# A decoder layer on one core: the self-attention's slot table rearranged, and two small operations moved from VectorE to GpSimd

## The chip, the cores and the metric

One core of one Trainium2 chip runs the whole program. The metric is device time in microseconds of that core. The kernel before was timed three times: 860.68, 863.87 and 865.61 us, median 863.87. Its profiled execution took 868.03 us, of which the profile spans 866.3 us. Engines are called by the profile's names: PE is TensorE, DVE is VectorE, ACT is ScalarE, POOL is GpSimd, SP is the sync engine, which here only issues transfers.

## The reference

Input `x` is 8 batches of 256 tokens of 512 numbers. Three stages follow each other: causal self-attention with 16 heads of 32 numbers, cross-attention with one head over 256 context rows and the tokens' own keys, and a mixture of 8 experts with one expert per token. The change touches the first stage alone:

```
h   = layernorm(x)                       # 8 x 256 x 512
qkv = h @ w_qkv                          # q, k, v of 16 heads x 32
p   = softmax(causal(q @ k.T / sqrt(32)))
x   = x + (p @ v) @ w_out
x   = x + cross_attention(layernorm(x)); x = x + experts(layernorm(x))
```

## The kernel before, in words

Float32 products are made in three passes: each operand is split into a high part, that TensorE multiplies fast, and a low part, the difference (`three_pass`, L51). ACT makes the high part out of PSUM by a cast, DVE the low part by a subtraction; for the probabilities and for v, POOL splits the rest once more (L322 to L324, L335 to L337).

The order of work is written out by hand. `self_attention` (L61) runs each batch in 16 slots, one for each head; all engines run the same list of slots and hand over by semaphores. In slot h, PE computes the scores S(h) of head h (L457). DVE takes the row maxima out of PSUM (L576), ACT takes the exponentials (L398). Two slots later PE transposes the probabilities (T, L470), ACT casts them (`pt_part[0]`, L408), one slot later DVE subtracts (`pt_rest`, L585) and POOL splits the rest (L335, L337). Every fourth slot, five slots behind the last head of a group of four, PE multiplies a group's probabilities by v (AV, `heads_by_values`, L488), and right behind it spreads the reciprocals of the row sums over PSUM by a product with the identity (L495). Before that DVE takes the reciprocals (L600) and copies them 32 wide (`rinv`, L603), three slots behind the last head. ACT copies the spread reciprocals (`r_sb`, L412), DVE multiplies (L590), ACT casts the product to `ot_hi` (L418), DVE subtracts to `ot_lo` (L594). `r_sb`, `o_sb` and `rinv` are one buffer, so that these steps follow each other strictly.

Beside heads, slots hold projection jobs on PE (`SLOTS`, L131): q0 to q3 and k0 to k3 (queries and keys of the four groups), u0, u1 and w0, w1 (values of the first and second half of the heads), X0, X1 (transposes of the normalised input), y0, y1 (output projection of the batch before). The job banks are two; a job waits until the job two before it has been taken out of PSUM. q and k go from `qk` to `stack` by SP transfers inside SBUF, since S wants high and low parts on top of each other: 12 transfers of 128 KB for half of the heads (`stack_half`, L252, L257), the second half when k3 is out, the first when k1 is. S waits for a head's own three transfers of those.

What the batches share: q0 to q2, k0 to k2, X and u of batch n+1 are made in batch n; a prologue makes those of batch 0 and, at its end, u0 and u1. Layer norm of the next batch is on DVE in slots 0 and 2 (L521 to L532), with one power on POOL in slot 1 (L315).

PE's order in a slot is S, AV, jobs, T. DVE's is the low part of the job before, maxima, `pt_rest`, output steps, reciprocals. ACT's is exponentials, the slot's own job, `pt_part`, output steps.

Of the kernel before, what the change touches and what calls it, by code (L numbers as in the profile page):

```python
# [60 lines left out]
def self_attention(nc, ident, x, w_qkv, w_out, x1, xin, xr, x1_out, x1_last_out, x1_first_in,  # L61
# [13 lines left out]
    HEAD_IN = 16 * 3  # L75
    NPROB, NPT, NREST = 4, 8, 4
    with ExitStack() as cx:
# [21 lines left out]
        r_sb = o_sb = rinv[:].rearrange("p q j d -> p (q j d)")  # L99
# [8 lines left out]
        stack = sb("stack", [3 * HD, 2, HG, 2, GH, S], F32R)  # L108
# [11 lines left out]
        stacked = [[sem(f"stacked_{half}_{j}") for j in range(HG)] for half in range(2)]  # L120
# [14 lines left out]
        PROLOGUE = ["X0", "X1", "q0", "k0", "q1", "k1", "q2", "k2", "u0", "u1"]  # L135
# [44 lines left out]

        def head_at(slot, lag, n):
# [16 lines left out]
        def v_at(j, n):  # L198

            return TB + n * V_JOBS + int(j[1]) + (0 if j[0] == "w" else TB)  # L200
# [44 lines left out]
        def _(sp):  # L245
# [6 lines left out]
            def stack_half(half):  # L252
                for j in range(HG):
                    for r, parts in enumerate((slice(0, 3, 2), slice(1, 3), slice(0, 4, 3))):
                        dst = stack[HD * r:HD * (r + 1), half, j, :, :, :].bitcast(F32)
                        src = qk[HD * j:HD * (j + 1), half, parts, :, :].bitcast(F32)
                        sp.dma_start(dst.rearrange("p w g s -> p w (g s)"),  # L257
                                     src.rearrange("p w g s -> p w (g s)")).then_inc(stacked[half][j], 16)

            def batch(n):  # L260

                wait(sp, job_ev, job_at("k3", n) + 1)
                sp.sem_inc(tick_sp, 1)
                if isinstance(n, int) and n == 0:
                    sp.wait_ge(w_split, 3)
                    sp.wait_ge(wo_split, 2)
                wait(sp, s_done, n * H)
                stack_half(1)
# [11 lines left out]
                if has("k1", n):  # L280
                    wait(sp, job_ev, job_at("k1", n) + 1)
                    sp.sem_inc(tick_sp, 1)
                    wait(sp, s_done, n * H + H // 2)
                    stack_half(0)
# [4 lines left out]
            wait(sp, job_ev, job_at("k1", -1) + 1)  # L289
            sp.wait_ge(w_split, 2)  # L290
            stack_half(0)
# [9 lines left out]
        def _(pool):  # L301
# [25 lines left out]
            def slot(n, h):  # L327
                if h == 1 and head_at(h, 0, n) is not None and (not isinstance(n, int) or n < B - 1):
                    next_rstd(n + 1)
# [9 lines left out]
                before = h - LO_JOB_LAG  # L339
                for j in jobs_of(before, n) if before >= 0 else jobs_of(H + before, n - 1 if isinstance(n, int) else n):  # L340
                    of = n if before >= 0 else n - 1
                    if j[0] in "uw" and not (isinstance(of, int) and of < 0):
                        v_lower_parts(j, of)

# [5 lines left out]
            for j in PROLOGUE:  # L350
                if j[0] == "u":
                    v_lower_parts(j, -1)
# [13 lines left out]
        def _(act):  # L366
            def evac(j, n):
# [3 lines left out]
                if j in ("q0", "q2"):  # L371
                    for s in stacked["q0 q2".split().index(j)]:
                        wait(act, s, (n + 1) * HEAD_IN)
                if j == "u0":
                    wait(act, av_done, n * G + GH if not isinstance(n, int) or n >= 0 else 0)
# [7 lines left out]
            for j in PROLOGUE:  # L383
# [4 lines left out]
                if j == "u0":  # L388
                    act.wait_ge(consts, CONSTS)
                evac(j, -1)  # L390

            def slot(n, h):
                e = head_at(h, 0, n)
# [7 lines left out]
                for j in jobs_of(h, n):  # L401
                    if j not in LATE:
                        evac(j, n)
                t = head_at(h, T_LAG, n)
                if t is not None:
                    act.wait_ge(t_done, n * H + h - T_LAG + 1)
                    wait(act, av_done, groups_before(h, T_LAG + NPT, n) + 1)
                    nc.scalar.copy(pt_part[0][:, t % NPT, :], t_ps[t % 2][:, 0:3 * P]).then_inc(pt_hi_done, 1)  # L408
                g = group_at(h, R_LAG, n)
                if g is not None:  # L410
                    act.wait_ge(r_done, groups_before(h, R_LAG, n) + 1)
                    nc.scalar.copy(r_sb, o_ps[g % 2][:, 1, :]).then_inc(rs_done, 1)  # L412
                g = group_at(h, ON_LAG, n)
                if g is not None:
                    if g == 0 and not (isinstance(n, int) and n < 1):
                        act.wait_ge(job_done, job_at("y1", n) + 1)
                    act.wait_ge(on_done, groups_before(h, ON_LAG, n) + 1)
                    nc.scalar.copy(ot_hi[:, g, :], o_sb).then_inc(ot_hi_done, 1)  # L418

# [11 lines left out]
        def _(pe):  # L431
            def job(j, n):
# [3 lines left out]
                if j == "q0":  # L436
                    pe.wait_ge(job_ev, job_at("X1", n) + 1)
                if j == "y0":
                    pe.wait_ge(ot_done, n * G)
# [4 lines left out]
            for j in PROLOGUE:  # L444
                if j in ("q0", "k0", "u0"):
                    pe.wait_ge(w_split, "qku".index(j[0]) + 1)
                job(j, -1)

            def slot(n, h):
                s = head_at(h, 0, n)  # L450
                if s is not None:
                    g, j = divmod(s, HG)
                    if s % (H // 2) < HG:
                        pe.wait_ge(stacked[g // GH][j], (n + 1) * HEAD_IN)
                    wait(pe, mx_done, n * H + h - 1)
                    for q in range(TB):
                        m = nc.tensor.matmul(s_ps[s % 2][:, q, :], stack[:, g // GH, j, 0, g % GH, q * P:(q + 1) * P],  # L457
                                             stack[:, g // GH, j, 1, g % GH, :], start=True, stop=True)
                    m.then_inc(s_done, 1)
                g = group_at(h, AV_LAG, n)  # L460
                if g is not None:
                    heads_by_values(g, h, n)
                for j in jobs_of(h, n):
                    job(j, n)
                t = head_at(h, T_LAG, n)
                if t is not None:
# [4 lines left out]
                    m.then_inc(t_done, 1)  # L471

            def heads_by_values(g, h, n):

                before, of = groups_before(h, AV_LAG, n), n if h >= AV_LAG else n - 1
                if g == 0:
                    pe.wait_ge(v_done, v_at("u1", of - 1) + 1)
# [34 lines left out]
        def _(dve):  # L512
            def norm_stats(k):
# [6 lines left out]
                for t in range(TB):  # L520
                    nc.vector.bn_stats(stats[:, t, :], xin[:, t, :]).then_inc(ln_dve, 1)  # L521
                for t in range(TB):
# [21 lines left out]
            norm_stats(0)  # L544
            norm_apply(0)
            for j in PROLOGUE:
# [5 lines left out]
                if j == "u0":  # L552
                    dve.wait_ge(consts, CONSTS)
                evac(j, -1)

            def slot(n, h):
                before = h - LO_JOB_LAG
                for j in jobs_of(before, n) if before >= 0 else jobs_of(H + before, n - 1 if isinstance(n, int) else n):
                    of = n if before >= 0 else n - 1
                    if isinstance(of, int) and of < 0:  # L560
                        continue
                    if j in LATE:
                        dve.wait_ge(job_done, job_at(j, of) + 1)
                        dve.wait_ge(xr_in, 16 * of)
                        xt = xr[:, int(j[1]), :]
                        nc.vector.tensor_tensor(xt, bank(j, of)[:, :], xt, ALU.add).then_inc(job_ev, 1)
                    else:
                        evac(j, of)
                s = head_at(h, 0, n)
                if s is not None:  # L570
# [9 lines left out]
                    m.then_inc(mx_done, 1)  # L580
                t = head_at(h, LO_LAG, n)
# [6 lines left out]
                if g is not None:  # L588
                    dve.wait_ge(rs_done, groups_before(h, ON_LAG, n) + 1)
                    nc.vector.tensor_tensor(o_sb, o_ps[g % 2][:, 0, :], r_sb, ALU.mult).then_inc(on_done, 1)  # L590
                g = group_at(h, OT_LAG, n)
                if g is not None:
                    dve.wait_ge(ot_hi_done, groups_before(h, OT_LAG, n) + 1)
                    nc.vector.tensor_tensor(ot_lo[:, g, :], o_sb, ot_hi[:, g, :].bitcast(F32),  # L594
                                            ALU.subtract).then_inc(ot_done, 1)
                g = group_at(h, RINV_LAG, n)
                if g is not None:
# [3 lines left out]
                    dve.wait_ge(rinv8_done, before + 1)  # L601
                    wait(dve, ot_done, before)
                    nc.vector.tensor_copy(rinv[:], free_ap(rinv8[:, g, :, :], 0, [[HG, TB], [1, HG], [0, HD]]))\  # L603
# [938 lines left out]
```

## Time and profile before

| | |
|---|---|
| median of 3 runs | 863.87 us (860.68 to 865.61) |
| profiled execution, its span | 868.03 us, 866.3 us |
| self-attention on PE | from 8.2 us to 391.98 us |
| busy over the span | PE 88%, DVE 61%, ACT 43%, POOL 36% |
| stretch 214 to 272 us, steady self-attention: busy of 58 us | PE 52.61, DVE 41.27, ACT 36.10, POOL 35.89; granted clock 1.00 |

A row of the order-of-time view has the start, the duration, the engine, the line of the kernel, the operation, output and inputs with sizes, and how many instructions are merged; in brackets stands how long the engine was idle before and who released it. Durations overlap: the next instruction may start before the last has ended, so the price of a step is here the distance from its start to the next start. Matmul ends are modelled. The granted clock is 1.00 at 2.4 GHz and 0.50 at 1.2 GHz.

### The profile page before, as it was taken

The page shows a single profiled execution, that of the slowest core. Times are in us where ns is not written, and L with a number is a line of the kernel's source. Part 1 is how long each engine was busy: PE and PEld are TensorE (multiplying, and loading weights), DVE is VectorE, ACT ScalarE, POOL GpSimd, SP SyncE. Part 2 cuts the span into 40 slices and gives each one's busy share as a digit, 9 for nine tenths or more (in the row PEclk, how much of TensorE's full clock was granted, in tenths as well). Part 3 has the DMA queues.
Part 4 walks back from the last instruction along what each step waited for, and adds up shares of the span by engine and source line. Part 5 has one row for each costly group of instructions (what it writes and reads, how often), then busy time and mean ns, then how long its engine had stood idle before and what let it go on. Part 6 is the DMA issues. An engine that isn't in the chain of part 4 may idle for free. (4 is left out here: it accounts for less than half of the span.)

```text
span 866.3 us, 19948 instructions
## 1 busy us (share of the span) xinstructions
PE 762.7 (88%) x6424; PEld 688.1 (79%) x6425; DVE 529.1 (61%) x1557; ACT 370.4 (43%) x1145; POOL 312.2 (36%) x456
## 2 busy tenths in 40 slices
PE   4798989898989999757999999999999985739995
PEld 4787979888888888646899998989899974637884
DVE  4678685868686867546565655556464533834664
ACT  4476675757575767534423232313133220622221
POOL 3376574757565656641000101010101101124662
PEclk9999999999999999879999999999999997868998
DMA  9643343444444434306712425060502111765630
GB/s 345 147 114 94 105 101 106 93 118 93 116 93 118 93 94 115 101 1 208 286 52 72 99 23 113 8 121 20 101 30 67 59 15 49 168 163 152 199 122 24
DMA packets 49575, 90.90 MB, mean 105 GB/s; under 512 B 11390, under 2 KB 11518, under 8 KB 49408
## 3 DMA queue, kind: packets, MB, share of 16 engines
q1 hardware_dynamic: 43872, 77.80, 34.2%
q0 software_dynamic: 5664, 12.61, 4.7%
q8 instruction: 21, 0.34, 0.2%
q14 instruction: 18, 0.15, 0.1%
HBM read 51.95 MB, written 18.77 MB: 82 GB/s over the span
## 5 line engine op out<-in xcount | busy, mean ns | idle before, releaser
L398 ACT ACTIVATE prob<-prob,nmax 128x128 f32<-128x128 f32 (+1 forms) x256 | 114.5, 448 | 77.9 <-DVE nmax L576 77.9
L337 POOL TENSOR_TENSOR pt_part<-pt_rest,pt_part 128x384 bf16<-128x384 f32 x128 | 117.8, 921 | 10.2
L335 POOL CAST pt_part<-pt_rest 128x384 bf16<-128x384 f32 x128 | 67.4, 527 | 113.5 <-DVE pt_rest L585 112.1
L576 DVE CUSTOM_DVE_ANT_0 prob<-a_s,mask 128x128 f32<-128x128 f32 (+1 forms) x256 | 80.2, 350 | 4.1 <-PE a_s L457 3.2
L585 DVE TENSOR_TENSOR pt_rest<-a_t,pt_part 128x384 f32<-128x384 f32 x128 | 70.8, 553 | 7.2 <-ACT pt_part L408 7.0
L408 ACT CAST pt_part<-a_t 128x384 bf16<-128x384 f32 x128 | 60.6, 473 | 32.3 <-PE a_t L470 32.1
L470 PE MATMUL a_t<-ident,prob 128*128 128x128 f32 x384 | 63.5, 275 | 12.2 <-DVE pt_rest L585 11.8
L457 PE MATMUL a_s<-stack 96*128 96x256 f32 x256 | 61.8, 324 | 0.2 <-DVE nmax L576 0.2
L470 PEld LDWEIGHTS a_t<-ident,prob 128*128 128x128 f32 x384 | 45.2, 141 | 17.9 <-issue 15.3
L488 PE MATMUL a_o<-pt_part,v_part 128*32 128x256 bf16 (+1 forms) x1536 | 40.4, 258 | 14.2 <-POOL pt_part L337 13.9
L922 ACT CAST b_kt_hi<-b_bank 128x256 fp32r<-128x256 f32 (+1 forms) x48 | 20.5, 445 | 66.1 <-PE b_bank L56 65.2
L488 PEld LDWEIGHTS a_o<-pt_part,v_part 128*32 128x32 bf16 x1536 | 31.9, 101 | 20.5 <-issue 9.9
L398 ACT ACTIVATION_READ_ACCUMULATOR prob<-prob,nmax 128x1 f32 x256 | 47.8, 187 | 0.0
L895 POOL TENSOR_TENSOR b_rstd<-b_veps,b_expo 128x2 f32<-128x2 f32 x8 | 5.6, 699 | 112.7 <-DVE b_veps L1070 112.7
L56 PE MATMUL a_job<-a_xt_hi,wqkv_hi 128*128 128x256 f32 x256 | 41.9, 287 | 2.6 <-DVE a_xt_lo L541 2.6
L891 POOL TENSOR_TENSOR b_rstd<-b_veps,b_expo 128x2 f32<-128x2 f32 x8 | 5.7, 708 | 106.7 <-DVE b_veps L1070 106.7
L56 PE MATMUL a_job<-a_xt_hi,wqkv_lo 128*128 128x256 f32 x256 | 40.4, 280 | 0.0
L56 PE MATMUL a_job<-a_xt_lo,wqkv_hi 128*128 128x256 f32 x256 | 40.3, 280 | 0.0
L541 DVE TENSOR_TENSOR qk<-a_job,qk 128x256 fp32r<-128x256 f32 x64 | 26.7, 421 | 21.4 <-ACT qk L380 21.3
L457 PEld LDWEIGHTS a_s<-stack 96*128 96x128 f32 x256 | 38.9, 192 | 0.4 <-issue 0.4
L56 PEld LDWEIGHTS a_job<-a_xt_hi,wqkv_hi 128*128 128x128 f32 x256 | 35.8, 194 | 3.0 <-issue 3.0
L1379 PE MATMUL c_bank<-ident,stage 128*128 128x128 f32 x128 | 21.5, 336 | 18.9 <-DMA stage<-in_w 16.8
(217 smaller groups left out, 1986.1 us busy)
## 6 DMA issues: line engine op xcount, KB each, us to landing
stack<-qk SPq DMA_DIRECT2D x192, 128.0 KB, 2.4
stage<-in_w SPq DMA_DIRECT2D x8, 1024.0 KB, 8.9
xin<-in_x SPq DMA_DIRECT2D x8, 512.0 KB, 3.6
xr<-in_x SPq DMA_DIRECT2D x8, 512.0 KB, 3.6
x<-xr SPq DMA_DIRECT2D x8, 512.0 KB, 2.8
xin<-x SPq DMA_DIRECT2D x8, 512.0 KB, 8.9
b_cin<-in_ctx SPq DMA_DIRECT2D x8, 512.0 KB, 3.5
xr<-x SPq DMA_DIRECT2D x8, 512.0 KB
```

The source lines that it names most:

```text
L56: ins = pe_matmul(out, a, b, start=first and i == 0, stop=last and i == len(steps) - 1)
L335: nc.gpsimd.tensor_copy(pt_part[1][:, t % NPT, :], rest).then_inc(pt_mid_done, 1)
L337: nc.gpsimd.tensor_tensor(pt_part[2][:, t % NPT, :], rest, pt_part[1][:, t % NPT, :], ALU.subtract).then_inc(pt_done, 1)
L398: a = nc.scalar.activation(prob[:, e % NPROB, cols], prob[:, e % NPROB, cols], ACT.Exp, scale=-1.0, bias=nmax[:, e, q:q + 1], accum_out=rs ...
L408: nc.scalar.copy(pt_part[0][:, t % NPT, :], t_ps[t % 2][:, 0:3 * P]).then_inc(pt_hi_done, 1)
L457: m = nc.tensor.matmul(s_ps[s % 2][:, q, :], stack[:, g // GH, j, 0, g % GH, q * P:(q + 1) * P], stack[:, g // GH, j, 1, g % GH, :], start ...
L470: m = nc.tensor.transpose(t_ps[t % 2][:, o:o + P], prob[:, t % NPROB, cols], ident[:])
L488: m = nc.tensor.matmul(o_ps[g % 2][j * HD:(j + 1) * HD, 0, seen], v_part[a][:, k, at:at + HD], pt_part[z][:, (g * HG + j) % NPT, cols], st ...
L541: m = nc.vector.tensor_tensor(lo, src, hi, ALU.subtract)
L576: m = nc.vector.tensor_tensor_reduce(out=prob[:, s % NPROB, cols], in0=s_ps[s % 2][:, q, 0:P * (q + 1)], in1=mask[:, P * (1 - q):], scale= ...
L585: nc.vector.tensor_tensor(pt_rest[:, t % NREST, :], t_ps[t % 2][:, 0:3 * P], pt_part[0][:, t % NPT, :], ALU.subtract).then_inc(pt_rest_don ...
L1379: m = nc.tensor.transpose(ring[i % RING][:, o * P:(o + 1) * P], stage[e % STAGED][:, o, c * P:(c + 1) * P], ident[:])
```

## The change

- `SLOTS` holds one job per slot: q3, k3, u0, u1, w0, w1, X0, X1, y0, y1, q0, k0, q1, k1, q2, k2 in slots 0 to 15. u0 and u1 now belong to their own batch, so the prologue has two jobs less.
- PE's order in a slot becomes S, T, AV, job. ACT takes a job out one slot later, first in its slot, and makes the exponentials last. DVE makes the maxima first, then the low part of the job before.
- `stack` is laid out by group. Each group has one semaphore for all its 12 transfers, each now 64 KB. There are 48 transfers per batch and SP issues a group when its k is out. S waits at a group's first head for all 12.
- The cast to `ot_hi` moves one slot later. `ot_lo` and the copy to `rinv` move from DVE to POOL, behind its probabilities and value parts. `r_sb` and `o_sb` get buffers of their own.
- Layer norm: statistics in slot 0, their aggregation in slot 2, the power on POOL in slot 3 (first in its slot), its use in slot 4.

```diff
-        SLOTS = {0: ["q3"], 2: ["k3"], 4: ["w0"], 5: ["w1", "X0"], 6: ["X1"], 7: ["y0"], 8: ["y1"], 9: ["q0"], 10: ["k0"],
-                 11: ["q1", "k1"], 12: ["u0"], 13: ["u1"], 14: ["q2"], 15: ["k2"]}
-        OWN, LATE = ("q3", "k3", "w0", "w1"), ("y0", "y1")
+        SLOTS = {0: ["q3"], 1: ["k3"], 2: ["u0"], 3: ["u1"], 4: ["w0"], 5: ["w1"], 6: ["X0"], 7: ["X1"], 8: ["y0"],
+                 9: ["y1"], 10: ["q0"], 11: ["k0"], 12: ["q1"], 13: ["k1"], 14: ["q2"], 15: ["k2"]}
+        OWN, LATE = ("q3", "k3", "u0", "u1", "w0", "w1"), ("y0", "y1")
...
-        T_LAG, LO_LAG, RINV_LAG, AV_LAG, R_LAG, ON_LAG, OT_LAG = 2, 3, 3, 5, 5, 6, 7
-        LO_JOB_LAG = 1
+        T_LAG, LO_LAG, RINV_LAG, AV_LAG, ON_LAG, OT_LAG = 2, 3, 3, 5, 6, 7
+        JOB_LAG = 1
-        EPILOGUE_SLOTS = 10
+        EPILOGUE_SLOTS = 11
+        STATS_AT, AGGR_AT, RSTD_AT, APPLY_AT = 0, 2, 3, 4
...
-            def stack_half(half):
+            def stack_group(g, n, early):
+
+                wait(sp, job_ev, job_at(f"k{g}", n) + 1)
+                sp.sem_inc(tick_sp, 1)
+                wait(sp, s_done, early)
                 for j in range(HG):
                     for r, parts in enumerate((slice(0, 3, 2), slice(1, 3), slice(0, 4, 3))):
+                        sp.dma_start(stack[HD * r:HD * (r + 1), g, j, :, :].bitcast(F32),
+                                     qk[HD * j:HD * (j + 1), g // GH, parts, g % GH, :].bitcast(F32))\
+                            .then_inc(stacked[g], 16)
...
 # SP, batch(n):
+                stack_group(2, n - 1, n * H - HG)
+                stack_group(3, n, n * H)
...
+                    stack_group(0, n, n * H + HG)
+                    stack_group(1, n, n * H + 2 * HG)
...
 # POOL, slot(n, h), behind the split of pt_rest:
+                for j, of in jobs_before(h, n):
+                    if j[0] in "uw":
                         v_lower_parts(j, of)
+                g = group_at(h, OT_LAG, n)
+                if g is not None:
+                    pool.wait_ge(ot_hi_done, groups_before(h, OT_LAG, n) + 1)
+                    nc.gpsimd.tensor_tensor(ot_lo[:, g, :], o_sb[:], ot_hi[:, g, :].bitcast(F32),
+                                            ALU.subtract).then_inc(ot_done, 1)
+                g = group_at(h, RINV_LAG, n)
+                if g is not None:
+                    before = groups_before(h, RINV_LAG, n)
+                    pool.wait_ge(rinv8_done, before + 1)
+                    pool.sem_inc(tick_pool, 1)
+                    wait(pool, r_done, before)
+                    pool.sem_inc(tick_pool, 1)
+                    nc.gpsimd.tensor_copy(rinv[:], free_ap(rinv8[:, g, :, :], 0, [[HG, TB], [1, HG], [0, HD]]))\
+                        .then_inc(rinv_done, 1)
...
 # PE, slot(n, h), behind S(h): T (two heads back), AV, then the job
-                    if s % (H // 2) < HG:
-                        pe.wait_ge(stacked[g // GH][j], (n + 1) * HEAD_IN)
+                    if j == 0:
+                        pe.wait_ge(stacked[g], (n + 1) * GROUP_IN)
```

## Rows read from the trace of the kernel before

**Rows 1.** Order of time, PE: S of slot 0 in batches 1, 4, 5, 7, and idle times

```profile
64.43 0.48 PE L457 MATMUL a_s<-stack 96*128 96x256 f32 x2
...
199.37 0.48 PE L457 MATMUL a_s<-stack 96*128 96x256 f32 x2
...
207.53 0.52 PE L470 MATMUL a_t<-ident,prob 128*128 128x128 f32 x3 [0.84 <-DVE pt_rest L585]
...
216.21 0.66 PE L208 MATMUL a_job<-ident,a_xn 128*128 128x128 f32 x4 [0.84 <-DVE v_rest L541]
216.70 0.49 PE L470 MATMUL a_t<-ident,prob 128*128 128x128 f32 x3
...
218.30 1.20 PE L56 MATMUL a_job<-wout_hi,ot_hi 128*128 128x512 f32 x4 [0.87 <-DVE ot_lo L594]
...
243.50 0.48 PE L457 MATMUL a_s<-stack 96*128 96x256 f32 x2
...
331.77 0.48 PE L457 MATMUL a_s<-stack 96*128 96x256 f32 x2
```

**Rows 2.** Order of time, PE: AV, y1, T, S, q0 and the next T

```profile
221.87 1.17 PE L488 MATMUL a_o<-pt_part,v_part 128*32 128x256 bf16 x48
...
223.44 1.18 PE L56 MATMUL a_job<-wout_hi,ot_hi 128*128 128x512 f32 x4
...
226.33 0.49 PE L470 MATMUL a_t<-ident,prob 128*128 128x128 f32 x3
226.58 0.48 PE L457 MATMUL a_s<-stack 96*128 96x256 f32 x2
226.90 0.63 PE L56 MATMUL a_job<-a_xt_hi,wqkv_hi 128*128 128x256 f32 x4
...
228.28 0.49 PE L470 MATMUL a_t<-ident,prob 128*128 128x128 f32 x3
```

**Rows 3.** Order of time, POOL: probabilities' split, values' split, and the power

```profile
239.74 0.51 POOL L335 CAST pt_part<-pt_rest 128x384 bf16<-128x384 f32 x1 [2.38 <-DVE pt_rest L585]
...
241.20 0.39 POOL L322 CAST v_part<-v_rest 128x256 bf16<-128x256 f32 x1
...
242.29 0.70 POOL L335 CAST pt_part<-pt_rest 128x384 bf16<-128x384 f32 x1
...
248.61 0.69 POOL L315 TENSOR_TENSOR a_rstd<-a_veps,a_expo 128x2 f32<-128x2 f32 x1
```

**Rows 4.** Order of time, DVE: low part, maxima, rest, output's low part; a late maximum

```profile
238.13 0.42 DVE L541 TENSOR_TENSOR v_rest<-a_job,v_part 128x256 f32<-128x256 f32 x1 [2.44 <-ACT v_part L380]
238.47 0.28 DVE L576 CUSTOM_DVE_ANT_0 prob<-a_s,mask 128x128 f32<-128x128 f32 x1
...
239.02 0.55 DVE L585 TENSOR_TENSOR pt_rest<-a_t,pt_part 128x384 f32<-128x384 f32 x1
...
241.86 0.76 DVE L594 TENSOR_TENSOR ot_lo<-rinv,ot_hi 128x256 fp32r<-128x256 f32 x1
...
368.45 0.29 DVE L576 CUSTOM_DVE_ANT_0 prob<-a_s,mask 128x128 f32<-128x128 f32 x1 [2.61 <-PE a_s L457]
```

**Rows 5.** Order of time, PE: the S for which that late maximum waited

```profile
367.74 0.48 PE L457 MATMUL a_s<-stack 96*128 96x256 f32 x2
```

**Rows 6.** Order of time, SP: the first stack transfers of all, and a half's twelve

```profile
20.90 23.08 SPq L257 DMA_DIRECT2D stack<-qk  x24
...
210.26 7.67 SPq L257 DMA_DIRECT2D stack<-qk  x12
```

**Rows 7.** Page, DMA issues: count, size of each, median us from issue to landing

```profile
stack<-qk SPq DMA_DIRECT2D x192, 128.0 KB, 2.4
```

**Rows 8.** Order of time, PE: batch 0's first S

```profile
29.26 0.60 PE L457 MATMUL a_s<-stack 96*128 96x256 f32 x2
```

**Rows 9.** Order of time, PE: an AV in batch 1 at the lower clock

```profile
74.36 2.11 PE L488 MATMUL a_o<-pt_part,v_part 128*32 128x256 bf16 x48 [0.85 <-POOL pt_part L337]
```

**Rows 10.** Busy time of PE in a stretch of batch 2: us, busy, clock, DMA share, GB/s

```profile
128.00:132.00 4.00, 3.40 (x8) 0.58 0.79 213
```

More of the change, by code:

```diff
@@ L119, in self_attention @@
         job_done, job_hi, job_ev = sem("a_job_done"), sem("a_job_hi"), sem("a_job_ev")
-        stacked = [[sem(f"stacked_{half}_{j}") for j in range(HG)] for half in range(2)]
+        stacked = [sem(f"stacked{g}") for g in range(G)]
         s_done, mx_done, ex_done = sem("s_done"), sem("mx_done"), sem("ex_done")
@@ L179, in jobs_of, with jobs_before, norm_at @@
             return [j for j in SLOTS.get(slot, []) if has(j, n)]
+        def jobs_before(slot, n):
+            t = slot - JOB_LAG
+            if t >= 0:
+                return [(j, n) for j in jobs_of(t, n)]
+            if isinstance(n, int) and n == 0:
+                return []
+            return [(j, n - 1) for j in jobs_of(H + t, n - 1 if isinstance(n, int) else n)]
+        def norm_at(slot, at, n):
+            return slot == at and (not isinstance(n, int) or n < B - 1)
         def head_at(slot, lag, n):
@@ L327, in slot @@
             def slot(n, h):
[L328 removed]
+                if norm_at(h, RSTD_AT, n):
                     next_rstd(n + 1)
@@ L368, in evac @@
                 act.wait_ge(job_done, job_at(j, n) + 1)
-                if j in ("q0", "q2"):
-                    for s in stacked["q0 q2".split().index(j)]:
-                        wait(act, s, (n + 1) * HEAD_IN)
+                if j[0] == "q":
+                    g = int(j[1])
+                    wait(act, stacked[g], (n if j in OWN else n + 1) * GROUP_IN)
                 if j == "u0":
-                    wait(act, av_done, n * G + GH if not isinstance(n, int) or n >= 0 else 0)
+                    wait(act, av_done, n * G - GH)
                 if j == "w0":
@@ L471, in slot @@
                     m.then_inc(t_done, 1)
+                g = group_at(h, AV_LAG, n)
+                if g is not None:
+                    heads_by_values(g, h, n)
+                for j in jobs_of(h, n):
+                    job(j, n)
             def heads_by_values(g, h, n):
@@ L551, in _ @@
                                             ALU.subtract).then_inc(w_split, 1)
-                if j == "u0":
-                    dve.wait_ge(consts, CONSTS)
                 evac(j, -1)
+            dve.wait_ge(consts, CONSTS)
             def slot(n, h):
[L557 to L568, printed above, removed]
                 s = head_at(h, 0, n)
@@ L580, in slot @@
                     m.then_inc(mx_done, 1)
+                for j, of in jobs_before(h, n):
+                    if j in LATE:
+                        dve.wait_ge(job_done, job_at(j, of) + 1)
+                        dve.wait_ge(xr_in, 16 * of)
+                        xt = xr[:, int(j[1]), :]
+                        nc.vector.tensor_tensor(xt, bank(j, of)[:, :], xt, ALU.add).then_inc(job_ev, 1)
+                    else:
+                        evac(j, of)
                 t = head_at(h, LO_LAG, n)
@@ L589, in slot @@
                     dve.wait_ge(rs_done, groups_before(h, ON_LAG, n) + 1)
[L590 to L595, printed above, removed]
+                    wait(dve, ot_done, groups_before(h, ON_LAG, n))
+                    nc.vector.tensor_tensor(o_sb[:], o_ps[g % 2][:, 0, :], r_sb[:], ALU.mult).then_inc(on_done, 1)
                 g = group_at(h, RINV_LAG, n)
```

108 lines of the change are left out of this document (43 added, 65 removed).

## The prediction

> **What bounds the kernel now.** I read the page first (PE is busy 88% of the span), then stretches of the busy-time table, then one whole batch in order of time on each engine, then SP's issues. The reader is to see that PE sets self-attention's pace, with holes. Batch 4 lasts from S at 199.37 us to S at 243.50, 44.13 us, and batches 5 and 6 last 88.27 together [rows 1]. PE's pieces, from start to start: T .25, S .32, a q, k, u or w job 1.38 (taken as 1.40, since one right behind AV starts slower), AV with the reciprocals 1.57, a y job 2.89 [rows 2], X .49 behind a wait [rows 1], taken as .47. A batch is 16 x .57 = 9.1, 12 jobs x 1.40 = 16.8, two y 5.8, two X .9, four AV 6.3 and about .2 of turn-over around each AV, .8: together 39.7 us without a hole. So holes cost 44.13 - 39.7 = 4.4 us per batch. They lie where slots are short: T waits for `pt_rest` (.84), X1 for the job bank (.84), y0 for `ot_lo` (.87) [rows 1], and two more like them. That is the most that any slot table can give: 4.4 x 8 = 35 us. No work is taken off PE by the change; it can only move holes.
>
> **The change, part by part.** The new slots without holes: 1.97 with a q, k, u or w job; 3.74 with an AV besides (slots 0, 4, 12); 1.04 with X (6, 7); 5.23 in slot 8 (AV, y0); 3.46 in slot 9. Again 39.7. The question is what is late in them.
>
> Regular slots. PE wants T at 1.97 + .32 = 2.29 us behind a slot's S, and T needs the `pt_rest` that DVE makes in the slot before. A waiting DVE starts its maxima .71 behind S (367.74 to 368.45) [rows 4, 5]; maxima take .55, the low part .34, and `pt_rest` started at 239.02 lets the next engine start at 239.74, .72 later [rows 3, 4]. That is 2.32: no hole worth counting (0 to .05 a slot). The holes of slots 1 to 4 go. ACT's and DVE's new order and the two operations taken off DVE are worth nothing beyond that, since DVE ends each slot before the next S; moved back, they would only lengthen slots in which DVE has room.
>
> POOL, slots 2 to 6. This is the first place where the change costs. A split of probabilities is 1.46 (239.74 to 241.20), of values 1.09 (241.20 to 242.29), the power .69 [rows 3]. The two new operations are not in the trace on POOL. `ot_lo` is a subtraction of 128x256 with two inputs: bounded below by the .39 of a cast of that size, above by what the 128x384 subtraction has of a split, 1.46 - .51 = .95; I take .70, what the subtraction of the same size has of the values' split (1.09 - .39). The copy to `rinv` is 128x256: at least the values' cast of .39, at most the .70 of the longest 128x384 cast shown; I take .50 with its waits. From slot 2 to slot 6, where the reciprocals of group 0 are spread, POOL has 5 splits 7.3, four value splits (u0, u1, w0, w1 now follow each other) 4.4, the power .7, `ot_lo` twice 1.4, the copy twice 1.0: 14.8 us. It can begin 2.32 behind slot 2's S and is never idle after that, so the copy is out 17.1 behind it. PE wants the reciprocals in slot 8, behind AV, at 1.97 + 1.97 + 3.74 + 1.97 + 1.04 + 1.04 + .57 + .1 + 1.1 = 13.5. Hole: 3.6 us per batch (2.8 to 4.5 by the bounds). The waits of T in the short X slots (DVE needs 2.2 in each against PE's 1.04) lie inside that hole: PE would wait anyway. Behind it are y0 and everything else on PE; y0's own need, `ot_lo`, comes before the copy.
>
> The Trainium skill speaks against this part: "GPSIMD Engine Reference", section "Engine selection", gives elementwise work to VectorE, with GpSimd about 2 times slower for two inputs. The trace has it milder: .70 for POOL's subtraction of 128x256 against .42 for DVE's [rows 3, 4]. By the page's factor `ot_lo` would be .84 and the hole 3.9 instead of 3.6.
>
> SP, slot 0. Second place. A batch's first S now waits for all 12 transfers of group 0, which SP may issue only when k0 (slot 11) is out in slot 12: .71 + .55 + .42 = 1.7 behind its S, with nothing else queued on SP then (the x transfers behind y1 are issued .5 us earlier). Twelve issues took 7.67 us, .64 apart [rows 6], and one lands 2.4 after its issue [rows 7]. The last lands at 1.75 + 11 x .64 + 2.4 = 11.2; PE is there after 3.74 + 3 x 1.97 = 9.65. Hole: 1.5 us. The size of each transfer is halved, its count of pieces is not. If issue were paid by bytes, the last would land at 7.7 and the hole would be 0; I take 1.5, because the issues after an idle time are .6 each too, with an empty queue. Group 1 follows at 9.4 and lands at 18.9; slot 4 comes at 20.9. Groups 2 and 3 have more room. 48 issues are 31 us of SP's 44.
>
> The Trainium skill, "DMA: Bandwidth & Descriptors", section "Anatomy of one DMA — SWDGE (gpsimd) path", has about 2 us fixed for a transfer, most of it the receipt of the write, plus bytes at 436 GB/s. By that half the bytes save .15 of the 2.4, and the hole would be 1.35; the trace has no stack transfer of that size.
>
> Steady batches: 39.7 + 3.6 + 1.5 = 44.8. Batches 1 to 6 now take 331.77 - 64.43 = 267.3 [rows 1]; 6 x 44.8 = 268.8, so +1.5.
>
> Clock. In batch 1 AV took 2.11 instead of 1.17 behind holes of .84 and .85 [rows 9], in batch 2 the clock was .58 in 128 to 132 us around y0 [rows 10]: the granted clock fell to 1.2 GHz after PE had sat idle in two or three short holes, and batches 1 to 3 took (199.37 - 64.43) - 3 x 44.13 = 2.6 us more for two falls, 1.3 each. The new slots 7 and 8 gather more idle time in one place (about .8, .8, .9 and 1.1, with 1.0, .3 and 1.1 of work between) than any spot of the steady batches before. I take four falls in six batches, 1.0 each, since part of the slow time lies beside waiting: +4 (0 to +10).
>
> Batch 0: SP may begin with k0 instead of k1, two jobs of 1.38 earlier than 20.90 [rows 6], at 18.2; group 0 lands at 18.2 + 7.0 + 2.4 = 27.6 against S at 29.26 [rows 8]: -1.7. u0 and u1 leave the prologue (2.8 us of PE), but PE waits for the stack there. Its end has the hole of slot 0, +1.5; POOL's backlog is smaller without older groups, and the hole in slot 8 replaces those of slots 3 to 7. I take -1.0 (-3 to +2). Batch 7 gets u0 and u1, in slots that stood nearly empty; y0 comes a slot later: +.5. At the very end `ot_lo` stands before the last y0, on POOL .70 instead of .42: +.3.
>
> Sum: 1.5 + 4 - 1.0 + .8 = +5.3, which puts the profiled execution of 868.03 at 873.3. That execution lies 4.2 us above the median of the three runs, 863.87, and the forecast is for the median: 863.9 + 5.3 = 869.
>
> **Rivals.**
> 1. The stack is paid by bytes: the hole in slot 0 is gone when issues are under (9.65 - 1.75 - 2.4) / 11 = .50 us apart. For: each transfer has half the bytes, and DMA queues were busy .79 in such a stretch [rows 10]. Against: .6 with empty queues. Price: 7 x 1.5 = 10.5, so 5.3 - 10.5 = -5.2: 858.7, faster. Chance .25.
> 2. The clock holds, for no single hole is much over 1.1 us: +1.3, 865. For: batches 4 to 6 held it with holes of .87. Chance .15.
> 3. POOL is later still: each new operation at its upper bound (hole 4.5, +.9 x 6 = 5) and a fall in every batch (+4 more): 5.3 + 5 + 4 = +14, 878. Chance .12.
> 4. The backlog on POOL doesn't reach AV, since some order that I misread lets PE go on: then only slot 0 and the short X slots cost, 42.5 a batch, 6 x 42.5 - 267.3 = -12 and no falls, 851. Chance .05.
> 5. The forecast, with 3 us of play to both sides: .43.
>
> **How the numbers follow.** What this kernel's measurement can tell from no change is about 0.5%, 4.3 us. Faster: 1 and 4, .30. Same: 2 and the lower third of the forecast, .28. Slower: the rest, .42. The range takes rival 1 with the clock held (854) and rival 3 (878).
>
> **What would show it.** Right: PE idle in slot 8 before the L495 products with the copy to `rinv` as releaser, some 3 us from T on; S of slot 0 idle 1.5 us behind the stack; no idle time in slots 1 to 5; POOL busy without a break from slot 2 to slot 6; granted clock below 1.00 near slot 8 in most batches; batches 44.8 us apart, or 46 with a fall. Wrong: stack issues under .5 us apart, a batch under 43.5 us, or idle time of PE in regular slots, which would mean that DVE or ACT have become the pace.

## The result, and the profile after

The changed kernel takes 870.57 us (median of 20 runs, 867.86 to 872.83), the kernel before 866.29 us in 20 runs beside them (860.48 to 871.51): a ratio of 1.0047 (95% interval 1.003 to 1.0064). The change costs some 4 us, where 5.3 were forecast. The profiled execution took 870.67 us (before: 868.03).

The profile after: its first line (busy time of each engine), then its groups for the heads' matrix products: line, engine, tiles, shapes and count, then busy us and mean ns of one, then the idle time in front of them and who ended it.

```profile
PE 767.7 (88%) x6424; PEld 692.8 (80%) x6425; DVE 502.6 (58%) x1493; ACT 379.3 (44%) x1145; POOL 340.6 (39%) x520
...
L489 PE MATMUL a_t<-ident,prob 128*128 128x128 f32 x384 | 65.0, 278 | 17.6 <-DVE pt_rest L607 16.9
L481 PE MATMUL a_s<-stack 96*128 96x256 f32 x256 | 54.6, 295 | 15.4 <-DMA stack<-qk 15.4
...
L512 PE MATMUL a_o<-pt_part,v_part 128*32 128x256 bf16 (+1 forms) x1536 | 41.1, 261 | 7.9 <-POOL pt_part L352 7.8
L519 PE MATMUL a_o<-ident,rinv 128*128 128x128 f32 x128 | 24.5, 317 | 6.5 <-POOL rinv L369 6.5
```

In these groups PE waits for four things: the stack's transfers in front of S (15.4 us), DVE's rest in front of T (16.9), POOL's probability parts (7.8) and POOL's spread reciprocals (6.5). The first and the last are new. Other waits shrank or went: y's first product waits 2.2 us for `ot_lo` where it waited 8.9, AV 7.8 for POOL instead of 13.9, and the 6.0 that X1 waited for its job bank are gone; T waits more, 16.9 instead of 11.8. Where they lie shows in order of time on PE: start, duration, and in brackets the idle time before.

```profile
28.04 0.80 PE L481 MATMUL a_s<-stack 96*128 96x256 f32 x2 [4.79 <-DMA stack<-qk]
...
34.16 0.40 PE L481 MATMUL a_s<-stack 96*128 96x256 f32 x2
...
48.02 2.11 PE L512 MATMUL a_o<-pt_part,v_part 128*32 128x256 bf16 x48 [0.77 <-POOL pt_part L352]
...
68.88 0.49 PE L481 MATMUL a_s<-stack 96*128 96x256 f32 x2 [2.28 <-DMA stack<-qk]
...
115.03 0.49 PE L481 MATMUL a_s<-stack 96*128 96x256 f32 x2 [2.33 <-DMA stack<-qk]
...
161.32 0.50 PE L481 MATMUL a_s<-stack 96*128 96x256 f32 x2 [1.16 <-DMA stack<-qk]
...
177.82 0.48 PE L481 MATMUL a_s<-stack 96*128 96x256 f32 x2
179.11 0.52 PE L489 MATMUL a_t<-ident,prob 128*128 128x128 f32 x3 [0.80 <-DVE pt_rest L607]
...
180.98 0.52 PE L489 MATMUL a_t<-ident,prob 128*128 128x128 f32 x3 [0.69 <-DVE pt_rest L607]
181.93 1.17 PE L512 MATMUL a_o<-pt_part,v_part 128*32 128x256 bf16 x48 [0.43 <-POOL pt_part L352]
184.04 0.71 PE L519 MATMUL a_o<-ident,rinv 128*128 128x128 f32 x4 [0.94 <-POOL rinv L369]
184.51 1.18 PE L56 MATMUL a_job<-wout_hi,ot_hi 128*128 128x512 f32 x4
...
206.00 0.50 PE L481 MATMUL a_s<-stack 96*128 96x256 f32 x2 [1.14 <-DMA stack<-qk]
```

These are the S of slot 0 in batches 0 to 4, in batch 0 also the S of slot 2 and an AV, and in batch 3 slots 7 and 8. Batch 3 lasts 206.00 - 161.32 = 44.68 us (44.13 before, [rows 1]); batches 4 to 6 differ from it by .14 at most. No hole is left in slots 1 to 5 of batch 3. Two queues answer for the two new waits, SP's issues and POOL in order of time:

```profile
18.77 32.69 SPq L273 DMA_DIRECT2D stack<-qk  x48
...
58.44 34.56 SPq L273 DMA_DIRECT2D stack<-qk  x48
...
104.91 32.51 SPq L273 DMA_DIRECT2D stack<-qk  x48
...
152.12 12.91 SPq L273 DMA_DIRECT2D stack<-qk  x20
```

```profile
169.37 0.50 POOL L350 CAST pt_part<-pt_rest 128x384 bf16<-128x384 f32 x1 [0.51 <-DVE pt_rest L607]
...
180.96 0.92 POOL L352 TENSOR_TENSOR pt_part<-pt_rest,pt_part 128x384 bf16<-128x384 f32 x1
...
182.93 0.72 POOL L360 TENSOR_TENSOR ot_lo<-o_sb,ot_hi 128x256 fp32r<-128x256 f32 x1
183.59 0.39 POOL L369 COPY rinv<-rinv 128x256 f32<-128x256 f32 x1
```

In batch 3 SP issues 20 transfers in 12.91 us, .65 apart, though each has 64 KB instead of 128. From its first issue to the S that waits for the twelfth it takes 161.32 - 152.12 = 9.20. POOL has no idle time from 169.37 to the end of the copy at 183.98, and this copy is the one that PE waits for at 184.04: 14.6 us of work in a row, 14.8 in the forecast.

**The whole kernel.** Self-attention's last y ends at 399.68 us, before at 392.14: +7.5. The remainder of the profiled execution, which the change doesn't touch, took 469.2 us after and 474.2 before, and 468.3 to 473.2 in the ten experiments below. Each trace is one execution, and the untouched remainder alone spreads by 6 us between them. So the +7.5 of the traces and the +4.3 of the medians can stand side by side, but how much of the +7.5 every execution has isn't known. From here on an experiment's gain is read in the timed ratio, and its cause in the batches of its trace.

### The profile page after: what moved, and what is told of

Read it like the earlier page. It is cut to its first block and busy times, and to the rows that moved or that the text cites. A ratio compares the mean times of both kernels' runs of the same rounds, so it can differ in the third digit from the quotient of the medians.

```text
span 868.9 us, 20202 instructions
## 1 busy us (share of the span) xinstructions
PE 767.7 (88%) x6424; PEld 692.8 (80%) x6425; DVE 502.6 (58%) x1493; ACT 379.3 (44%) x1145; POOL 340.6 (39%) x520
## 5 line engine op out<-in xcount | busy, mean ns | idle before, releaser
L350 POOL CAST pt_part<-pt_rest 128x384 bf16<-128x384 f32 x128 | 64.6, 504 | 89.0 <-DVE pt_rest L607 88.8
L489 PE MATMUL a_t<-ident,prob 128*128 128x128 f32 x384 | 65.0, 278 | 17.6 <-DVE pt_rest L607 16.9
L481 PE MATMUL a_s<-stack 96*128 96x256 f32 x256 | 54.6, 295 | 15.4 <-DMA stack<-qk 15.4
L489 PEld LDWEIGHTS a_t<-ident,prob 128*128 128x128 f32 x384 | 42.4, 141 | 23.9 <-issue 17.7
L481 PEld LDWEIGHTS a_s<-stack 96*128 96x128 f32 x256 | 40.9, 193 | 18.2 <-issue 10.5
L56 PE MATMUL a_job<-a_xt_hi,wqkv_hi 128*128 128x256 f32 x256 | 47.4, 310 | 2.8 <-DVE a_xt_lo L567 2.8
L404 ACT CAST qk<-a_job 128x256 fp32r<-128x256 f32 x64 | 23.6, 368 | 32.8 <-PE a_job L56 32.5
L1377 ACT CAST c_xt_hi<-c_bank 128x512 fp32r<-128x512 f32 x23 | 13.5, 587 | 55.2 <-PE c_bank L1412 55.2
```

What stands on the lines that cost most here:

```text
L56: ins = pe_matmul(out, a, b, start=first and i == 0, stop=last and i == len(steps) - 1)
L350: nc.gpsimd.tensor_copy(pt_part[1][:, t % NPT, :], rest).then_inc(pt_mid_done, 1)
L404: e = nc.scalar.copy(hi, src)
L481: m = nc.tensor.matmul(s_ps[s % 2][:, q, :], stack[:, g, j, 0, q * P:(q + 1) * P], stack[:, g, j, 1, :], start=True, stop=True)
L489: m = nc.tensor.transpose(t_ps[t % 2][:, o:o + P], prob[:, t % NPROB, cols], ident[:])
```

## The experiments

Nearly all edit the changed kernel. Times are medians; in parentheses the ratio to the kernel before, timed beside it on the same chip, with its interval.

**e1: a semaphore for each head's stack.** PE waits for a head's own 3 transfers, as the kernel before did, and no longer for the group's 12.

```diff
-                            .then_inc(stacked[g], 16)
+                            .then_inc(stacked[g][j], 16)
...
-                    if j == 0:
-                        pe.wait_ge(stacked[g], (n + 1) * GROUP_IN)
+                    pe.wait_ge(stacked[g][j], (n + 1) * HEAD_IN)
```

> The changed kernel, with a semaphore for each head's three stack transfers, as the kernel before had it; nothing else differs. Theory (the hole in front of a batch's first S is the wait for all twelve transfers of group 0): PE's idle time before S of slot 0 goes, 1.2 to 1.3 us in batches 3 to 7 and 2.3 in batches 1 and 2, 10.6 us in all, and nothing behind it was waiting too, so self-attention ends 10 to 11 us earlier and the whole lies about 860, 0.7% under the kernel before. Rival (that wait only stands in front of another one, POOL's backlog or DVE): slot 8 gets longer by what slot 0 loses, and the time stays within 3 us of 870.6.

852.73 us (.9846, .9815 to .9876): 18 us, more than the holes alone. Order of time on PE: S of slots 0 and 2 in batch 0, S of slot 0 in batch 1, X0 of batches 3 and 4.

```profile
24.51 0.50 PE L481 MATMUL a_s<-stack 96*128 96x256 f32 x2 [1.12 <-DMA stack<-qk]
...
28.74 0.40 PE L481 MATMUL a_s<-stack 96*128 96x256 f32 x2
...
59.76 0.40 PE L481 MATMUL a_s<-stack 96*128 96x256 f32 x2
...
163.09 0.60 PE L222 MATMUL a_job<-ident,a_xn 128*128 128x128 f32 x4
...
206.38 0.60 PE L222 MATMUL a_job<-ident,a_xn 128*128 128x128 f32 x4
```

The batch now lasts 206.38 - 163.09 = 43.29 us, 1.4 less, with the holes around slot 8 as they were (.75, .68, .49 and .95 behind the X0 at 163.09); no S waits after the first. The first S starts 3.5 earlier, and batch 0 takes 35.25 (24.51 to 59.76) instead of 40.84. Of the 5.6 us some 2.4 are the hole before the next S(0). Nearly all of the others lie where the clock is low in the kernel after: 1.9 in slots 0 and 1 (28.04 to 34.16, against 24.51 to 28.74) and 1.1 around the AV at 48.02. The clock shows in the stretch 28 to 32 of the kernel after and of e1 (us, busy of PE, PEld, DVE, ACT, POOL, granted clock, DMA share, GB/s):

```profile
28.00:32.00 4.00, 3.96 (x18) 3.96 (x19) 1.84 (x6) 1.36 (x5) 0.00 (x0) 0.50 0.40 96
```

```profile
28.00:32.00 4.00, 4.00 (x37) 4.00 (x37) 2.73 (x18) 3.39 (x13) 0.70 (x1) 1.00 0.31 75
```

After 4.79 us without work PE had 1.2 GHz, after 1.12 it had 2.4 GHz. The other traces agree for the first S: the granted clock fell in all five runs that waited 2.8 to 4.8 us for it (the kernel after, e2, e3, e6, e11) and in none of the five that waited .8 to 1.6 (e1, e7 to e10). The second fall, at the AV at 48.02, is not shown to be the hand-over's: e6 has the same first wait (4.80) and keeps its clock there.

**e2: both operations back on VectorE.** The two blocks that the change put on GpSimd (`ot_lo`, `rinv`) stand in VectorE's slot again; all else stays.

> The changed kernel, with ot_lo and the copy to rinv back on DVE in the same slots; nothing else differs. Theory (POOL's backlog from slot 2 to slot 6 sets slot 8): POOL has 2 x (0.68 + 0.35) = 2.1 us less before slot 8. AV waits for the last split of group 0 a little less (its idle 0.43 goes), the products of the reciprocals don't wait (0.94 goes), y0 doesn't wait. DVE gets 0.34 to 0.7 for each ot_lo and 0.3 for each copy; in slot 2 (with the norm's aggregation) and slot 6 (before the short slot 7) that delays T by up to 0.6 each. Net 0.5 to 1.2 us per batch less, 4 to 8 us in all, about 864. Rival (the move to POOL is what holds this slot table together, since DVE has no room in slots 2 and 6): T's holes in slots 3 and 7 grow by 1 us or more each, and the time is at or over 870.6.

876.05 us (1.0115, 1.008 to 1.0149): slower by 5.5, and the rival was right. Order of time on PE, a batch's slots 0, 4 and 8:

```profile
159.88 0.50 PE L467 MATMUL a_s<-stack 96*128 96x256 f32 x2 [0.71 <-DMA stack<-qk]
...
171.02 0.52 PE L475 MATMUL a_t<-ident,prob 128*128 128x128 f32 x3 [1.03 <-DVE pt_rest L593]
...
181.44 0.52 PE L475 MATMUL a_t<-ident,prob 128*128 128x128 f32 x3 [1.56 <-DVE pt_rest L593]
```

POOL's holes are gone from the steady batches, and T's waits for DVE rise from 16.9 to 32.5 us in the whole trace. In slot 8 the hole grows from .69 to 1.56: T needs the rest that DVE makes one slot earlier, and now `ot_lo`, the copy and the low part of X0's job follow each other on DVE in front of it.

**e3: the spread first in GpSimd's slot.** The copy to `rinv` stands ahead of the V parts and of `ot_lo`.

> The changed kernel, with POOL's copy to rinv put in front of the values' split and of ot_lo in its slot; nothing else differs. Theory (in slot 8 the reciprocals are the last thing POOL delivers, behind 1.09 of values and 0.68 of ot_lo): the 0.94 us idle before the products of the reciprocals goes, ot_lo comes 0.35 later and y0 then waits for it some 0.3 to 0.5. Net 0.4 to 0.6 us per batch, 3 to 4 us in all, about 867. Rival (AV's own wait for POOL is what counts, and the queue behind it is as long in any order): nothing moves, 870.6 within 1.5 us.

869.2 us (1.0033, 1.0012 to 1.0054), 1.4 less; the interval overlaps that of the change. Order of time on PE, slot 8:

```profile
178.87 1.17 PE L512 MATMUL a_o<-pt_part,v_part 128*32 128x256 bf16 x48 [0.48 <-POOL pt_part L352]
181.06 1.19 PE L56 MATMUL a_job<-wout_hi,ot_hi 128*128 128x512 f32 x4 [0.38 <-POOL ot_lo L369]
```

The wait of .94 is gone, and .38 for `ot_lo` stands in its place: reordering a full queue passes most of the wait on. A batch of this trace takes 44.30 us, .4 less than 44.7, the lower end of what the theory gave; the gain in the medians is not clear of noise.

**e5: GpSimd's part alone, on the kernel before.** The old slots and hand-overs, with only `ot_lo` and the spread moved.

> The kernel before, with only one part of the change: ot_lo and the copy to rinv made on POOL behind its other work of the slot, and r_sb and o_sb in buffers of their own. Slot table, stack and orders are those of before. Theory (a hand-over to POOL must be two slots ahead of its use): in slot 6 POOL has a split of 1.46 and a values' split of 1.09 in front of ot_lo, so that y0 in slot 7 starts about 3 us later than with DVE's (POOL was through with both at 220.65 in batch 4, y0 started at 218.30), and the reciprocals of the groups come at most 1 us late elsewhere: +2.5 to +3.5 us per batch, 20 to 25 in all, about 889. Rival (DVE is relieved by 3.5 us per batch and T's holes shrink with it): at most +5 us in all.

898.93 us (1.0378, 1.0344 to 1.0412), 32 us slower. The group of y's first product in the whole trace, and one of its waits:

```profile
L56 PE MATMUL a_job<-wout_hi,ot_hi 128*128 128x512 f32 x64 | 24.4, 514 | 30.8 <-POOL ot_lo L347 30.8
```

```profile
234.80 2.07 PE L56 MATMUL a_job<-wout_hi,ot_hi 128*128 128x512 f32 x4 [3.96 <-POOL ot_lo L347]
```

On POOL, in order of time, the split ahead of `ot_lo` and `ot_lo`:

```profile
231.41 0.50 POOL L335 CAST pt_part<-pt_rest 128x384 bf16<-128x384 f32 x1 [0.45 <-DVE pt_rest L600]
...
233.95 0.72 POOL L347 TENSOR_TENSOR ot_lo<-o_sb,ot_hi 128x256 fp32r<-128x256 f32 x1
```

In the old table y0 stands in slot 7, directly behind both X slots. This is no backlog: POOL sat idle for .45 us before the probabilities' split at 231.41. It is the order within the slot: that split and the values' split come first, and POOL starts `ot_lo` only at 233.95. Part of the 32 us is the clock, since the product behind the wait takes 2.07 instead of 1.18. The same two operations on POOL are worth -5.5 us in the new table and +32 in the old.

**e6: the backlog taken away.** The middle and low parts of w0 and w1 are made in slots 8 and 9, where POOL is idle, not in 5 and 6; nothing is left out.

```diff
                 for j, of in jobs_before(h, n):
-                    if j[0] in "uw":
+                    if j[0] == "u":
                         v_lower_parts(j, of)
+                w = {8: "w0", 9: "w1"}.get(h)
+                if w is not None and (not isinstance(n, int) or n < B):
+                    v_lower_parts(w, n)
```

> The changed kernel with one edit: GpSimd makes the middle and low parts of w0 and w1 in slots 8 and 9, where it stood idle, and not in slots 5 and 6 (nobody reads them before the next batch's use of group 2's heads). Theory (the holes in slot 8 are GpSimd's backlog of slots 2 to 6): the products' wait for probability parts (0.43) and for the spread reciprocals (0.94) go in every batch, 1.4 x 8 = 11 us less at most, some 9 after what stands behind them; time about 861. The waits of X0's and X1's slots (0.80 and 0.69, for VectorE's rest) stay. Rival (VectorE sets these slots by itself and GpSimd is only level with it): the hole moves to the T products or to the wait for VectorE's reciprocal, and the time stays within 2 us of the changed kernel's, 869 to 871.

858.71 us (.993, .9904 to .9957), 12 less than the change. PE's groups, whole trace:

```profile
L515 PE MATMUL a_o<-pt_part,v_part 128*32 128x256 bf16 (+1 forms) x1536 | 40.9, 260 | 3.7 <-POOL pt_part L352 3.5
L522 PE MATMUL a_o<-ident,rinv 128*128 128x128 f32 x128 | 24.1, 313 | 0.0
```

```profile
174.54 0.41 POOL L372 COPY rinv<-rinv 128x256 f32<-128x256 f32 x1
```

```profile
175.62 0.71 PE L522 MATMUL a_o<-ident,rinv 128*128 128x128 f32 x4
```

Both waits of the steady batches are gone (what is left lies in batch 0 and the last one), and nothing took their place. The copy, in order of time on POOL, is out at 174.95, .7 before PE wants it. A batch takes 43.1 us instead of 44.7. So POOL's two holes in slot 8 were its backlog, and they go though both new operations stay on POOL.

**e7: both cures.** e1 and e6 together.

> Both edits: a semaphore for each head's stack (the first S of a group waits for 3 transfers, not 12) and the lower parts of w0 and w1 in slots 8 and 9. Theory: the two holes have different causes and places, so the gains add up: 852.7 less some 9, about 843. Rival: with the hole of slot 0 gone the job of slot 8 or the stack's own transfers come late, and the gains overlap: 848 or more.

842.19 us (.9737, .9701 to .9773), as the sum of the two said. X0 of two batches:

```profile
158.81 0.60 PE L222 MATMUL a_job<-ident,a_xn 128*128 128x128 f32 x4
...
200.54 0.60 PE L222 MATMUL a_job<-ident,a_xn 128*128 128x128 f32 x4
```

41.73 us a batch: 1.56 less than e1's, for holes of .49 and .95, which the idle column gives as 1.44.

**e8: the rest first.** e7, and VectorE makes T's rest ahead of the job's low part in each slot (the block of `pt_rest` moved above the loop over the jobs).

> As the one before, and VectorE takes the rest of T's product ahead of the job's low part in each slot. Theory: the rest is ready 0.34 to 0.61 earlier, so the T products' waits in X0's and X1's slots (0.75 and 0.68) shrink to about 0.4 and 0.1: 1 us per batch, 7 to 8 in all, about 836. Rival: the low part is what the next job's bank or SP's transfers wait for; it comes 0.55 later, and a job's product or the S of a group waits in its place: no gain, or a loss of up to 5, 843 to 848.

834.11 us (.9645, .961 to .968): the fastest, 36 us under the changed kernel and 31 under the one before.

```profile
155.81 0.60 PE L222 MATMUL a_job<-ident,a_xn 128*128 128x128 f32 x4
157.13 0.52 PE L492 MATMUL a_t<-ident,prob 128*128 128x128 f32 x3 [0.48 <-DVE pt_rest L602]
...
158.55 0.52 PE L492 MATMUL a_t<-ident,prob 128*128 128x128 f32 x3 [0.23 <-DVE pt_rest L602]
...
196.33 0.60 PE L222 MATMUL a_job<-ident,a_xn 128*128 128x128 f32 x4
```

A batch takes 40.52 with .71 of idle time in it; that leaves 39.8, close to the prediction's floor of 39.7.

**e9: the spread first, without the backlog.** e7 with e3's edit.

> As e7, and GpSimd spreads the reciprocals ahead of the V parts and of the output's low part in its slot. Theory (with the backlog gone GpSimd reaches the spread in time in either order): no more than 1 us from e7's time. Rival (the wait for the spread is its place in the slot's order and not the backlog): in e7 the 0.94 stays, and here it goes, 5 to 7 us less than e7.

842.69 us (.9739, .9702 to .9776), e7's time: with POOL in time its order within a slot is worth nothing.

**e10: the new table alone.** e1 and e2 together, so the slots and the halved transfers are all that is left of the change.

> The changed kernel with the other two parts of the change taken out: a semaphore for each head's stack as before, and the output's low part and the spread of the reciprocals on VectorE as before. What stays of the change is the table of slots, its lags, and the stack's layout with half the bytes per transfer. Theory: the hand-over per group costs what it did in e1 (17.8), here too: 876 - 18 = 858, so the table alone is 8 us faster than the kernel before. Rival: VectorE sets the pace of every slot with the two operations on it, the waits for its rest (32 us of idle time on PE in that kernel) grow where the hole of slot 0 goes, and the time stays at 866 or more: the table is worth nothing without GpSimd's part.

865.55 us (.9969, .9934 to 1.0003). The theory's 858 fell, and the time is the rival's; the interval takes in no difference from the kernel before. Order of time on PE:

```profile
167.91 0.60 PE L222 MATMUL a_job<-ident,a_xn 128*128 128x128 f32 x4
...
172.23 0.52 PE L475 MATMUL a_t<-ident,prob 128*128 128x128 f32 x3 [1.55 <-DVE pt_rest L593]
...
212.41 0.60 PE L222 MATMUL a_job<-ident,a_xn 128*128 128x128 f32 x4
```

A batch takes 44.50, more than the 44.13 of before; the shorter prologue, by which the first S starts at 24.66 and not at 29.26 [rows 8], pays it back. (The trace is of an execution of 860.18 us.) The hand-over per group costs 1.0115 - .9969 = .0146, 12.6 us here against 17.8 with POOL's part: its hole in slot 0 is .64 to .81 in batches 3 to 7 of e2 and 1.14 to 1.30 in the changed kernel. From SP's first issue to that S it takes 9.21 in e2 and 9.20 in the changed kernel (batch 3 of each), so it is PE that comes later to slot 0 there, behind more waits for DVE.

**e11: the hand-over per group, on the kernel before.** There the first S of a half waits for all four heads' transfers.

> The kernel before with one edit: the S of a half's first head waits for all four heads' stack transfers (12), and not for its own 3. Theory: in the old order too twelve issues 0.64 apart and 2.4 to land (190.69 + 7.7 + 2.4 = 200.8 in batch 4) come 1.4 behind the S at 199.37; in batch 0, where they are 0.96 apart, 20.9 + 10.6 + 2.4 = 33.9 is 4.6 behind the S at 29.26: 7 x 1.4 + 4.6 = 14 us, with a fall of the clock in batch 0 some 2 more, 881. Rival: the old kernel's holes in slots 1 to 4 and its waits of group 0's reciprocals take the late S up, so that less than 5 us are left: 871 or less.

880.65 us (1.0114, 1.0078 to 1.0151): 10 us slower by the ratio, 12 by the medians, of 14 expected. The group, and two of the waits:

```profile
L458 PE MATMUL a_s<-stack 96*128 96x256 f32 x256 | 63.5, 332 | 12.0 <-DMA stack<-qk 10.4 <-DVE nmax L577 1.7
```

```profile
31.25 0.77 PE L458 MATMUL a_s<-stack 96*128 96x256 f32 x2 [2.79 <-DMA stack<-qk]
...
205.95 0.49 PE L458 MATMUL a_s<-stack 96*128 96x256 f32 x2 [0.92 <-DMA stack<-qk]
```

The wait is .9 in batches 3 to 6 and not 1.4, and 2.8 in batch 0 and not 4.6. The trace is of the fastest execution, 872.19 us, so it shows the waits but not the whole cost. The hand-over by group costs time in the old table too.

**Together**, as ratios to the kernel before, each of the table, the hand-over and POOL's part with the others as named:

```
                          hand-over per head   hand-over per group
old table                      1.000                1.011  (e11)
old table, POOL's part         1.038  (e5)          not run
new table                       .997  (e10)         1.012  (e2)
new table, POOL's part          .985  (e1)          1.005  (the change)
... and w later                 .974  (e7)           .993  (e6)
```

The traces stand in the same order: against the changed kernel self-attention ends 13.9 us earlier in e6, 19.6 in e1, 31.4 in e7 and 39.2 in e8.

## Why the prediction was right, step by step

- **Regular slots without a hole: right.** No wait over .1 stands in slots 1 to 5 of batch 3, against .84 and less before [rows 1], and such a slot takes 1.98 us (165.12 to 167.10) where 1.97 was taken.
- **POOL's backlog: right, in place and size.** Forecast: 3.6 us between the X slots and y0. From the S at 177.82 to y0 at 184.51 are 6.69 us. The same steps without waits start .24, .35, .36, .24, .44, 1.10 and .47 apart (in slots that don't wait, and in e6 for the products), 3.2 together: 3.5 of holes. The brackets show 2.86; each hole costs .1 to .25 more than its bracket, since a piece before a hole counts its whole duration (.48) where the next piece otherwise starts .24 or .35 behind it. The brackets give POOL 1.37 of it and DVE 1.49, but the text's reading that T's waits lie inside a hole that PE would have anyway holds: POOL has no idle time from 169.37 on, so the part that AV needs is out at 181.88 (180.96 + .92) whenever T comes, and AV starts at 181.93. The price of the backlog and the gain from taking it away are therefore not the same. With POOL in time T's waits stay (16.5 us in e6), a batch gets only 1.6 shorter and not 3.5, and e8 gets at more of the rest. `ot_lo` starts .68 and the copy .35 before what follows, where .70 and .50 were taken; that makes POOL's queue .3 shorter than forecast.
- **The stack in slot 0: right in mechanism, nearly in size.** Forecast 1.5, shown 1.14 to 1.30, and 1.4 with the restart. Issues stay .64 to .65 apart, which refutes rival 1 (paid by bytes). The issue to landing is 2.0, not 2.4. The section "Anatomy of one DMA — SWDGE (gpsimd) path" in "DMA: Bandwidth & Descriptors" of the Trainium skill gives bytes at 436 GB/s beside a fixed part, by which half the bytes save an estimated .15 of the 2.4; the traces show .4. Its formula is for transfers issued by GpSimd, and these are issued by SP. e1 and e11 show the wait to be the cost.
- **A steady batch: 44.8 forecast, 44.7 measured.** e8's 40.52 with .71 idle supports the floor of 39.7, on which this rests.
- **The clock: wrong.** Four falls in six batches were taken (+4); there was one, and not where the text had it: at slot 0 of batch 2, behind the hole of 2.33 (granted clock .57 in 116 to 120), while the hole of 2.28 in front of batch 1 had none. It made batch 2 46.29 us long, 1.6 more than a steady one; +4 was forecast. The holes of .80, .69, .43 and .94 within 6 us left the clock at 2.4 GHz in all of batches 1 to 6; in e1 it fell behind the first three of them in two of the six, batches 2 and 6 (.64 in 124 to 128, .69 in 296 to 300). No rule for it follows from these runs. In the number of falls rival 2 (none) was nearer than the forecast.
- **The S of batches 1 and 2: not foreseen.** From SP's first issue to the S it takes 68.88 - 58.44 = 10.44 and 115.03 - 104.91 = 10.12 us, against 9.20 in batch 3 (9.44 by the forecast's terms), and slot 0's hole is 2.3 instead of 1.2. The one in front of batch 2 makes batch 1 longer (46.15 us): 1.2 that the text didn't have, where its +4 for the clock was 2.4 too much. In each of these stretches the trace has packets that load instructions, in the one of batch 3 none:

```profile
q8 instruction: 1, 0.02, 0.7%
q14 instruction: 1, 0.01, 0.3%
```

  (The queues' part for 104 to 118 us: packets, MB, share.) That SP's issues paused for them was not tested and stays open.
- **Batch 0: the step that failed.** Forecast -1.0, measured 68.88 - 64.43 = +4.45 [rows 1]. The start was nearly right: the stack was forecast for 27.6, and S starts at 28.04 instead of 29.26 [rows 8]. The text says that PE waits for the stack there, but gives that wait no price in the clock: PE is idle for 4.79 us, the clock falls, S and q3 run at half speed, and an AV at 48.02 again takes 2.11. Against e1 these cost 1.9 and 1.1 us. Against the forecast .9 more go by the hole of 2.28, .5 by the start (1.2 gained and not 1.7) and .9 by the smaller holes: batch 0 takes 35.25 in e1, without the hand-over, and 35.17 before, and the text had taken .8 off for them. e1 shows the first fall and the hole to be the hand-over's; for the fall at 48.02 that stays open (e6).
- **The end: -.9 against +.8.** Why it got shorter was not looked into. The sum of self-attention in the traces is thus +4.0 in batches 1 to 6 (5.5 forecast) plus 4.45 minus .9, +7.5 against 5.3, and +4.3 in the medians. The two big terms of a steady batch were right. That the total agrees so well (869 forecast, 870.57 measured) is partly luck: the clock's term was too high, batch 0's too low by 5.5, the late S was missing, and single executions differ by more than what is left.
- **The Trainium skill against POOL.** "GPSIMD Engine Reference" of the Trainium skill, "Engine selection", gives such work to VectorE. For the single operation the traces agree in direction: `ot_lo` takes .73 on POOL on the mean and .44 on DVE in e2, a factor of 1.7 where the Trainium skill has about 2. (The .42 with which the prediction compared is DVE's subtraction for `v_rest`; `ot_lo` itself took .54 on the mean in the kernel before, and .76 in [rows 4].) For the kernel e2 measures the opposite (5.5 us slower on VectorE) and e5 the Trainium skill's side (32 us slower on GpSimd): the slot table decides.

## What to carry to other kernels

A hand-over by group makes the first consumer wait for the last transfer, and here the price was largest at the start, where PE's wait of 4.79 us was followed by the lower clock: count issues times pitch plus landing for each consumer's own data, and signal each part by itself if its consumer can start on it. When an operation is moved to an idle engine, lay that engine's work of the surrounding slots end to end: its busy share (39%) says nothing about a backlog of 15 us, and an item that nobody waits for yet is the one to move out of the way. Two edits with holes in different places add up (e1, e6, e7); two in the same full queue pass one wait to and fro (e3).

## What the runs showed of the hardware

- A transfer of 64 KB within SBUF lands 2.0 us after its issue and one of 128 KB after 2.4 [rows 7], but SP issues both .64 us apart: with halved bytes and doubled count its time for the same data doubles (48 issues in 32.5 to 34.6 us per batch, as SP's rows of after show).
- PE's granted clock was .50 right after 4.79 us of idle time, and 1.00 after 1.12 us at the same place (e1). In the kernel after it fell behind 2.33 us and stayed behind 2.28, and four holes under 1 us, 2.9 us together within 6, left it at 1.00 in six batches of six; in e1 it fell in two of six behind the first three.
- A subtraction of 128x256 into fp32r takes POOL .73 us on the mean (DVE .44 in e2), and a copy of the same size that spreads reciprocals .40 (DVE .30), no more than POOL's cast of that size (.43).
